# A decoder layer with 14 experts: on GpSimd, the scatter of one tile and the reciprocal deviation of the next change places

## The reference, cut to what matters

```python
x = _layernorm(x + _L0_attn_ref(x, W_qkv, W_out))
x = _layernorm(x + _L0_xattn_ref(x, ctx, ctx, Wq, bq, Wk, bk, Wv, bv, Wo, bo))
x = _layernorm(x + _L0_ffn_ref(x, router_w, w1, b1, w2, b2))

def _L0_ffn_ref(h, router_w, w1, b1, w2, b2):      # x: 4096 tokens x 256
    logits = x @ router_w                          # 14 experts
    assignments = argmax(logits)                   # each token: one expert
    weights = softmax(logits)[assignments]
    hid = gelu(x @ w1[e] + b1[e])                  # 256 -> 512, for its expert e
    moe_out = (hid @ w2[e] + b2[e]) * weights      # 512 -> 256

def _layernorm(x, eps=1e-05):
    return (x - mean(x)) / sqrt(var(x) + eps)
```

## Time and profile before

| what | us |
|---|---|
| median of three runs | 639.02 |
| lowest, highest | 635.59, 640.14 |
| span of the profiled execution, first to last instruction | 595.6 |
| median less span | 43.4 |
| TensorE busy in the span | 563.3 (95%) |
| VectorE busy | 463.4 (78%) |
| GpSimd busy | 405.4 (68%) |
| ScalarE busy | 343.1 (58%) |

### The profile page before, as it was taken

One profiled execution on the slowest core, in us unless ns is written; L12 is line 12 of the kernel. 1 busy time (PEld: TensorE's weight loads), 2 busy tenths in 40 slices (PEclk: granted clock), 3 DMA queues, 4 the chain that ended last, 5 costly groups with the idle time before them and its releaser, 6 DMA issues.

```text
span 595.6 us, 16640 instructions
## 1 busy us (share of the span) xinstructions
PE 563.3 (95%) x5608; PEld 476.7 (80%) x5608; DVE 463.4 (78%) x1071; ACT 343.1 (58%) x842; POOL 405.4 (68%) x554
## 2 busy tenths in 40 slices
PE   7989999999999999999999999799979999999990
PEld 6777788788888788788788778568869999999990
DVE  2779999999999899999999989865455566555561
ACT  1456666666676576665766766546625555555540
POOL 4346675678778678677678766776777677777652
PEclk9799999999999999999999999969989999999996
DMA  7415125125414314413714201114273333333200
GB/s 207 149 42 181 24 51 194 28 68 147 76 47 150 76 50 109 132 33 89 168 26 136 68 7 41 32 39 119 55 102 97 90 81 89 96 92 91 68 16 0
DMA packets 76692, 50.11 MB, mean 84 GB/s; under 512 B 39222, under 2 KB 70970, under 8 KB 76608
## 3 DMA queue, kind: packets, MB, share of 16 engines
q1 hardware_dynamic: 71264, 40.60, 26.8%
q0 software_dynamic: 5344, 8.44, 5.6%
HBM read 40.55 MB, written 10.60 MB: 86 GB/s over the span
## 4 chain that ended last, share of the span: by engine, by line
PE 74%; POOL 9%; issue 7%; DVE 5%; ACT 2%; DMA 1%; POOLq 0%; ACTq 0%; DVEq 0%
PE ps_r L822 15%; PE ps_r L740 13%; PE ps_s L956 10%; PE ps_r L972 10%; PE ps_r L807 5%; PE ps_r L902 5%; PE ps_s L762 4%; PE ps_s L753 3%; POOL token_lists L1579 3%; PE ps_r L795 2%; POOL prob L1498 2%; PE ps_r L879 2%; PE ps_r L897 2%; PE ps_r L904 2%; POOL out L1605 1%
## 5 line engine op out<-in xcount | busy, mean ns | idle before, releaser
L1498 POOL TENSOR_TENSOR prob<-prob,rden 128x616 f32<-128x616 f32 (+1 forms) x96 | 138.3, 1447 | 58.3 <-DVE rden L1173 56.6
L999 ACT COPY probT<-ps_r 128x512 f32<-128x512 f32 x192 | 86.8, 480 | 43.3 <-PE ps_r L740 41.4
L1141 DVE TENSOR_REDUCE mx<-ps_s 128x8 f32<-128x616 f32 (+1 forms) x96 | 88.8, 925 | 21.7 <-PE ps_s L753 14.9
L1019 ACT ACTIVATE prob<-prob 128x616 f32<-128x616 f32 (+1 forms) x96 | 79.4, 833 | 33.9 <-DVE prob L1152 33.9
L1161 DVE TENSOR_REDUCE den<-prob 128x8 f32<-128x616 f32 (+1 forms) x96 | 88.3, 921 | 6.9 <-ACT prob L1019 5.7
L1152 DVE TENSOR_TENSOR prob<-ps_s,mx 128x616 f32<-128x616 f32 (+1 forms) x96 | 89.8, 936 | 4.5 <-PE ps_r L740 3.0
L740 PE MATMUL ps_r<-ident,prob 128*128 128x128 f32 (+1 forms) x576 | 88.4, 281 | 1.6 <-POOL prob L1498 1.0
L956 PEld LDWEIGHTS ps_s<-xgT,w1b 128*128 128x128 f32 x720 | 87.2, 192 | 2.4 <-issue 0.3
L972 PE MATMUL ps_r<-w2s,hT 128*128 x360 | 86.7, 385 | 1.3 <-DVE yb L1401 1.1
L956 PE MATMUL ps_s<-xgT,w1b 128*128 128x128 f32 x720 | 87.9, 275 | 0.2 <-ACT xgT L1107 0.2
L740 PEld LDWEIGHTS ps_r<-ident,prob 128*128 128x128 f32 (+1 forms) x576 | 66.1, 142 | 16.8 <-issue 9.6
(11 more groups left out here) (158 smaller groups left out, 1011.0 us busy)
## 6 DMA issues: line engine op xcount, KB each, us to landing
w1s<-in_w SPq DMA_DIRECT2D x14, 512.0 KB
w2s<-in_w SPq DMA_DIRECT2D x14, 512.0 KB
b2r<-in_b SPq DMA_DIRECT2D x45, 128.0 KB, 3.2
xT<-in_x_cols SPq DMA_DIRECT2D x16, 256.0 KB, 2.9
xres<-in_x SPq DMA_DIRECT2D x16, 256.0 KB
x_rows<-x2s SPq DMA_DIRECT2D x32, 128.0 KB, 1.9
xkT<-in_xk_cols SPq DMA_DIRECT2D x16, 128.0 KB, 2.7
ctxT<-in_ctx_cols SPq DMA_DIRECT2D x16, 77.0 KB, 2.1
```

The lines of the kernel that those rows point to most:

```text
L999: nc.scalar.copy(probT[0:rows, par, first:last], src[0:rows, 0:last - first]).then_inc(pT_copied[kind].sem, 1)
L1019: nc.scalar.activation(prob[:, n % 3, 0:width], prob[:, n % 3, 0:width], ACT.Exp, scale=SCALE).then_inc(exp_done[kind].sem, 1)
L1141: nc.vector.tensor_reduce(m, s, axis=AX, op=ALU.max).then_inc(max_done[kind].sem, 1)
L1498: nc.gpsimd.tensor_tensor(p, p, rden[:, par, 0:heads, None].to_broadcast([P, heads, width]), ALU.mult).then_inc(scaled[kind].sem, 1)
```

## The change

In the string for GpSimd's tiles the last two entries change places. A round now reads: gather of tile k + 6, scatter of tile k - 1, `pow` of tile k. No instruction, wait, buffer or DMA is added or taken away. `pow` of tile 0 stays where `POOL_LAST` has it.

```diff
         PE_TILES = "y@2 hid@0 rows@-1"
         ACT_TILES = "wa@-2 rows@-2 gelu@-1"
         DVE_TILES = "eps@1 bias@0 wd@-4 res@0 stat@0 norm@1 agg@0"
-        POOL_TILES = "gather@-3 pow@3 put@4"
+        POOL_TILES = "gather@-3 put@4 pow@3"
         SP_TILES = "slots@-2 bias_row@-2"
```

## The result

The changed kernel took 639.56 us, median of 22 runs (635.17 to 643.07), against 638.19 us in 22 runs of the kernel before beside them (633.35 to 641.68). The ratio is 1.005, with a 95% interval of 1.0026 to 1.0075. On 638.19 us that is +3.2 us, between +1.7 and +4.8 us. The two medians lie 1.4 us apart and the two means 1.7 us, less than the ratio says, so the size of the shift is known only roughly.

The account below looks back on a forecast made before the run. TensorE was taken to bound the steady rounds, and GpSimd alternating with VectorE the tail. Steady rounds 0, change-over 0 and tail +2.0 us gave 641.0 us, range 635.0 to 645.0 us.

Parts of the forecast that it names:

- The tail: After TensorE's last matmul: `pow` queues behind scatters that start 0.80 us after `norm`; last scatter later, +2.0 us.
- The steady rounds: Tiles 12 to 43: TensorE sets 3.73 us a tile, GpSimd's round needs 3.18 us; no change, 0.
- The slack of 0.41 us: Steady rounds: `pow` ends 1.34 us later, yet 0.41 us before VectorE is free to start `norm`.
- The change-over: Around 428 to 441 us: bias 1.35 us later, hidden under TensorE's pause, which shrinks from 3.50 to 2.15 us; 0.
- Rival A: Change-over: SP's bias row no longer delays tile 8's gather, pause vanishes, clock kept; -3.5 us, 637.5 us with tail; chance 0.20.
- Rival B: Steady rounds: scatter preparation not hidden, GpSimd bounds at 4.29 us a round; +18 us, 659 us with tail; chance 0.05.
- Rival C: Change-over: TensorE's clock drops earlier, during the 2.4 us wait; +1 us, 642.0 us with tail; chance 0.07.
- Rival D: Tail: nothing visible, the scatter starts within 0.2 us; 639.2 us; chance 0.10.
- with the 43.4 us around it: Whole kernel: 43.4 us, the difference to the median, added to the predicted 597.6 us span, giving 641.0 us.

Follow-up runs that it names:

- run 1: Kernel before, with the scatter in front of `pow` only in the rounds from 42 on; 640.82 us against 636.39 us, ratio 1.0038.
- run 6: Changed kernel plus two small idle additions on GpSimd before the scatter, tiles 8 to 36; no time given, 148.8 us from gather of tile 8 to TensorE's last matmul.
- run 9: The changed kernel, unaltered, profiled once more on the same chip as run 5; 640.41 us, one run.
- run 10: Changed kernel plus one small idle addition on GpSimd before the scatter, tiles 8 to 36; no time given, one tile of 3.90 us, tail 6.85 us.
- run 2: Changed kernel with the old order again from round 42 on; ratio 0.9919 against the kernel before, means 635.29 and 636.33 us.
- run 3: Kernel before, with the scatter in front of `pow` only in the rounds up to 11; ratio 0.9999.
- run 5: The kernel before, unaltered, profiled a second time; 635.49 us, one run.
- run 7: Kernel before plus two small idle additions on GpSimd before `pow`, tiles 8 to 36; no time given, 150.7 us from gather of tile 8 to TensorE's last matmul.
- run 11: The same kernel as run 3 (new order only in the rounds up to 11) on another chip; ratio 1.0018.
- run 4: Kernel before, with the scatter in front of `pow` but of a tile one earlier (put@5 instead of put@4); ratio 1.0026.

## Why the prediction was right, and where not

The predicted sign and the class (within 1%) came true, and 641.0 us lies 1.4 us above the median. The shift against before, +2.0 predicted, was measured as +3.2 us (+1.7 to +4.8) by the ratio and +1.4 us by the medians. That the total came so near is partly luck, since two terms that were put at 0 were not 0 and had opposite signs. By steps:

**The tail: right, mis-sized by 0.3 to 0.6 us.** Its start of 0.80 us, borrowed from a gather that waits, was 0.81 to 0.82 us. Runs 1, 6, 9 and 10 give +2.30 to +2.31 us; in these and in after the scatter of 42 took 1.24 or 1.25 us where 1.03 was assumed (+0.21). The profile of after gives +2.58: `pow` of tile 42, which the working left at its old place, stood behind a late scatter of 41 there, and `norm` of 42 starts 0.10 us before TensorE's end where the working, and runs 1, 6, 9 and 10, have 0.34 to 0.36 us (+0.26). For that profile the working started one tile too late.

**The steady rounds: the step that failed.** "The bounds of this term are therefore 0 and 0 ... and I take 0 for all 32 tiles." It came to +1.2 and +1.5 us in the two profiles of after and +1.07 in run 2, and to 0 in each profile that keeps the old order there (before, runs 1, 3, 5, 7, 11), and in run 6. The slack of 0.41 us holds as long as the residual sums come every 3.73 us: `pow` ends 3.8 us behind its own sum, and `norm` can start 4.2 us behind it if the next sum keeps its time. In after the sums end 2.64 to 5.00 us apart, and `norm` waited for `pow` in 13 of about 30 rounds, up to 0.7 us. The prediction's own sign, "the prediction is wrong if a steady tile takes longer than 3.73 us", was met by seven tiles.

What TensorE waits for is in the rows. In 31 of the 32 longer tiles (seven in after, five in run 2, eleven in run 4, eight in run 9, one in run 10) the first weight load of the w1 product starts 0.11 to 0.12 us behind the end of ScalarE's copy of the transposed rows. That copy starts 1.55 to 1.84 us behind the transposes' weight load there, and 0.52 to 0.53 us in every steady tile of before and of runs 1, 3, 5, 6, 7 and 11. The exception is a tile of 3.78 us in run 9.

Why ScalarE's copy and VectorE's w1 copy come late stays open: by its records TensorE is done with the transposes up to 1.1 us before. A late `norm` is not shown as the cause either. Runs 4 and 6 exclude the simple answers: in run 4 the scatter's `norm` is a round older and the loss is largest, in run 6 `pow` ends just before `norm` in every round and there is none.

**The change-over: right in shape, one consequence missed.** List entry to scatter 0.31 us (0.30), bias 1.32 us later (1.35), landing unchanged. The w2 product waited 1.79 us (2.4 predicted), and the pause was 1.39 us (2.15). What the term of 0 left out is that a shorter pause kept the clock. Both profiles of before, and runs 1 and 7, which have the old order here, have a stretch near 0.5 behind a pause (0.50 in the earlier trace rows, 0.58 in run 5's 476 to 480), where a w2 product takes 3.0 to 3.4 us (before, runs 5 and 7); seven profiles with the new order have none, and theirs takes 1.9 us. On the third distance less longer tiles, that is 148.9 (after), 149.0 (run 2), 148.8 (run 3) and 148.8 us (run 6) against 150.5 and 150.2 us (before, run 5): a gain of 1.2 to 1.7 us. It shows only where VectorE's w1 copy meets no `remote` wait in the change-over. In the four profiles that have one, of 1.4 to 4.2 us, the distance is 150.5 and 150.7 us by the old order (runs 1 and 7) and 150.4 and 150.2 us by the new one (runs 4 and 9). Runs 10 and 11 are at 147.6 and 147.7 us on a chip of which there is no profile of before, so their last 1.1 us is not ascribed to anything.

**Rival A fell by its cause and half held by its consequence.** The bias row of SP no longer stands beside the gather (474.43 against 473.31 in after), and the rows still reach TensorE 7.0 to 7.1 us after its issue, in after and in runs 2 and 3 (6.6 us in run 9, 6.7 in the old order on the same chip). The other load had not held them up. The turns that the queues take at a DMA engine, which the Trainium skill has in "DMA: Bandwidth & Descriptors", section "SWDGE vs HWDGE vs iDMA", give no gain here. The 1.4 us that A booked for the kept clock did come.

**Rival B** (4.29 us a round) fell: the scatter starts 0.31 us behind the gather and 0.57 us of `pow` right behind it. A VectorE copy beside the scatter did not block it for its own length; run 6 has the w1 copy at 542.53 within a scatter of 1.03 us. That bears on the port rule of the Trainium skill, "SBUF — State Buffer", section "Who interferes with whom": not seen in this place, though no run shows in which mode the copy ran. **Rival C** (clock falls earlier) fell: 1.79 us of waiting left the clock where it was. **Rival D** fell with the 0.81 us.

**The sum.** After against before by the distances: tail +2.6, tiles +1.2, change-over -1.6, so +2.2 us. Run 9 against run 5: tail +2.3, tiles +1.5, change-over 0, so +3.8 us. The runs say +3.2 us by the ratio, +1.7 by the means and +1.4 by the medians. All of that agrees in sign and in a size of roughly 1.5 to 4 us, and no more closely. The step "with the 43.4 us around it" was a misreading (1.7 us lie around a span; the rest was the five pauses and half-clock stretches that this execution did not have), which did no harm since the shift was taken against the median anyway; it would have, had a term been scaled by the span.

**Is there a better order?** The change-over alone has the distances of a gain of 1.4 to 1.7 us (run 3) and nothing lost elsewhere, but its times can't be told from before in either comparison (runs 3 and 11). It is not claimed. A `pow` moved to VectorE, which would take the alternation out of the tail, wasn't tried.

## What to carry to other kernels

Where two engines hand one tile back and forth and nothing else is left, put the short operation that the other engine waits for in front of a DMA issue that must wait for a result only just made: that issue costs its start (0.8 us here) and its length (1.0 us), and everything queued behind pays both, once per tile. A round is not safe because each single wait has slack: ask whether the rounds still repeat evenly, and count starts, since a window in which the bound engine is "busy" can hide longer tiles. Check the name that a trace gives to a wait against what the program waits for. Before two spans are compared, compare the pauses and the granted clock stretch by stretch; a shorter pause can also keep the clock up, and is then worth more than its own length.

## What the runs showed of the hardware

- In the attention part, from 140 to 380 us, TensorE's granted clock falls to 0.50 for 3.4 to 10.2 us at a time, always within 5 us of the start of a pause of TensorE. The pauses are 1.7 to 3.8 us long, and 53 to 56 us apart in after. One profile of before has neither the pauses nor the falls, all others have both. Two pauses of 1.7 us (197 us, runs 6 and 11) left the clock up.
- The times follow the mean granted clock: over the 112 runs of before and of runs 1 to 4 and 11, on two chips, by about 4.5 us per 0.01 of it, with 1.1 us of scatter left. That is most of the spread of about 10 us between runs of one kernel. At equal clock before is 1.3 us faster on one chip than on the other. At equal clock and on the same chip, run 4 stands at +2.0 over before, run 1 at +1.3, run 2 at +1.2, run 3 at +0.1 and run 11 at -0.2 us (each ± 0.8). For after this can't be said, as the clocks of the 22 runs of before beside it are not on record. The comparison takes away a part of what is looked for, since a longer idle tail and a kept clock change the mean clock as well.
- A gather issued behind eight list entries took 7.0 us to reach TensorE with SP's bias row beside it or not (before, after), twice the 3.4 us of the steady rounds. On the chip of runs 10 and 11 the same gather was through within 5.9 us, and TensorE's transposes show no wait for it.
- One idle operation of 0.20 us in front of a scatter in tiles 8 to 36 went with a steady part 1.0 to 1.3 us shorter (0.17 us of longer tiles instead of 1.2 and 1.5), one profile each on different chips.
